# Splitting the SiLU of the last stage of a LayerNorm, convolution, attention and gate kernel into two activations

## The reference, cut to what matters

```
xn = layernorm(x)                                   # x: 2 x 4096 x 4096, f32
s  = attention(conv3(xn)) @ proj_w + proj_b         # conv 4096 -> 3*1024, 16 heads, blocks of 128 rows
g  = silu(xn * w_sum + w_dense @ expert_bias)       # top 8 of 64 router weights, w_sum their sum
x  = x + s * g
```

## Time and profile before

| what | value |
|---|---|
| median of 2 runs | 1908.17 us (1907.36 to 1908.99) |
| the profiled execution, its own time | 1908.72 us |
| span of its slowest core, core 1 | 1907.2 us |
| spans of the 8 cores | 1888.7 to 1907.2 us |
| PE busy | 1539.2 us, 81% of the span |
| DVE busy | 374.1 us, 20% |
| ACT busy | 381.8 us, 20% |
| POOL busy | 214.3 us, 11% |

### The profile page before, as it was taken

The page is one execution under the profiler, slowest core; times in us unless marked ns, Lnnn a source line. Parts: engine busy times, 40 slices in busy tenths (PEclk is TensorE's granted clock), DMA queues, the critical chain, the costliest instruction groups (busy, mean ns, idle before and its releaser), DMA issues.

```text
span 1907.2 us, 17823 instructions; the slowest of 8 cores (1888.7 to 1907.2 us)
## 1 busy us (share of the span) xinstructions
PE 1539.2 (81%) x7424; PEld 727.6 (38%) x7424; DVE 374.1 (20%) x644; ACT 381.8 (20%) x445; POOL 214.3 (11%) x180
## 2 busy tenths in 40 slices
PE   0345799999999999999999999886765773966780
PEld 0345344444444444444444444333443441311220
DVE  2776100000000000000000000003255231533543
ACT  1443000000000000000000000596345331423322
POOL 0000011111111111111111111000000000221133
PEclk9877799999999999999999999997555556876685
DMA  5997666666666666666666666441000048044224
GB/s 138 218 248 158 76 78 78 76 76 74 75 76 77 78 78 76 73 74 76 77 77 78 77 74 85 75 66 23 1 1 1 1 89 187 1 124 141 89 94 170
DMA packets 230821, 163.62 MB, mean 86 GB/s; under 512 B 74691, under 2 KB 222403, under 8 KB 226499
## 3 DMA queue, kind: packets, MB, share of 16 engines
q0 software_dynamic: 155472, 92.97, 38.4%
q1 hardware_dynamic: 75270, 69.50, 13.8%
HBM read 220.69 MB, written 16.78 MB: 125 GB/s over the span
## 4 chain that ended last, share of the span: by engine, by line
PE 61%; DMA 12%; DVE 10%; ACT 7%; POOL 3%; issue 3%; SPq 3%; POOLq 0%; DVEq 0%; ACTq 0%
PE pCv L632 53%; DMA AL<-x 7%; PE pWO L913 4%; DMA AL<-pw 4%; POOL AL L1047 2%; ACT AL L694 2%; DVE AL L787 1%; DVE AL L1030 1%; PE pQ L716 1%; DVE tStat L320 1%; SPq L416 1%; ACT AL L1042 1%; DVE tRs L779 1%; ACT L694 1%; POOL AL L1050 1%
## 5 line engine op out<-in xcount | busy, mean ns | idle before, releaser
L632 PE MATMUL pCv<-AL 128*128 128x512 bf16 x4608 | 1002.9, 380 | 1.0 <-DVE tWmT L550 1.0
L632 PEld LDWEIGHTS pCv<-AL 128*128 128x128 bf16 x4608 | 450.0, 98 | 553.8 <-issue 4.4
L765 DVE TENSOR_REDUCE tSc<-pS 128x1 f32<-128x512 f32 x32 | 21.8, 680 | 1189.9 <-PE pS L758 1189.9
L575 POOL DMA_DIRECT2D AL<-cw x144 | 125.9, 875 | 1053.4 <-PE pCv L632 863.0
L647 ACT ACTIVATE AL<-pCv,tCbT 128x512 bf16<-128x512 f32 x48 | 29.1, 688 | 889.2 <-PE pCv L632 889.2
L454 PE MATMUL pLgT<-AL 128*64 128x128 bf16 x768 | 62.0, 262 | 124.6 <-DMA AL<-AL 124.6
L982 PE MATMUL pPr<-AL 128*128 128x512 bf16 x448 | 120.8, 418 | 17.3 <-DVE AL L1030 17.3
L913 PE MATMUL pWO<-AL 64*128 64x256 bf16 x512 | 109.8, 414 | 5.7 <-DVE AL L839 5.7
L454 PEld LDWEIGHTS pLgT<-AL 128*64 128x64 bf16 x768 | 60.9, 141 | 125.5 <-issue 125.5
L913 PEld LDWEIGHTS pWO<-AL 64*128 64x128 bf16 x512 | 73.2, 144 | 41.4 <-issue 6.6
L799 PE MATMUL pPT<-tI,AL 128*128 128x128 bf16 x128 | 18.7, 301 | 73.1 <-DVE AL L787 73.1
(11 more groups left out here) (94 smaller groups left out, 843.4 us busy)
## 6 DMA issues: line engine op xcount, KB each, us to landing
AL<-cw POOLq DMA_DIRECT2D x144, 512.0 KB, 5.9
AL<-x SPq DMA_DIRECT2D x16, 2048.0 KB, 13.9
out<-AL SPq DMA_DIRECT2D x8, 2048.0 KB, 8.8
AL<-pw POOLq DMA_DIRECT2D x8, 1024.0 KB, 8.5
AL<-wq POOLq DMA_DIRECT2D x1, 2048.0 KB, 18.8
AL<-wk POOLq DMA_DIRECT2D x1, 2048.0 KB, 15.1
AL<-wv POOLq DMA_DIRECT2D x1, 2048.0 KB, 14.8
AL<-wo POOLq DMA_DIRECT2D x1, 2048.0 KB, 15.7
```

What stands on the lines that cost most here:

```text
L575: sCWs[gi % 4].add(e.dma_start(out=cwr[:, gi % 4, :].rearrange("p (g f) -> p g f", g=8), in_=d_cw[s, g].rearrange("g p f -> p g f")), 16)
L632: ins = e.matmul(p_cv[:, 512 * (bs + 2 * sub + hf): 512 * (bs + 2 * sub + hf) + 512], lhsT, xnTh[:, o:o + 512], start=(step == 0), stop=(s ...
```

## The change

SiLU of a tile is issued as two activations. The first covers columns 0 to 1535 and waits for the first three segments only (3 x 512 columns); the second covers columns 1536 to 4095 and waits for all eight. `cSIL` now goes up by two in a tile: POOL's product waits for the first activation, DVE's for the second.

```diff
                 @AC
                 def _(e, tt=tt):
+                    e.wait_ge(cGI.h, 8 * tt + 3)
+                    cSIL.add(e.activation(gw[:, 0:1536], gw[:, 0:1536], AF.Silu), 1)
                     e.wait_ge(cGI.h, 8 * (tt + 1))
-                    cSIL.add(e.activation(gw, gw, AF.Silu), 1)
+                    cSIL.add(e.activation(gw[:, 1536:4096], gw[:, 1536:4096],
+                                          AF.Silu), 1)
 
                 @GP
                 def _(e, tt=tt):
-                    e.wait_ge(cSIL.h, tt + 1)
+                    e.wait_ge(cSIL.h, 2 * tt + 1)
                     cPL.add(e.tensor_mul(s6[tt % 2][:, 0:1536], s6[tt % 2][:, 0:1536],
                                          gw[:, 0:1536]), 1)
...
                 @DV
                 def _(e, tt=tt):
-                    e.wait_ge(cSIL.h, tt + 1)
+                    e.wait_ge(cSIL.h, 2 * tt + 2)
                     dedge(e, e.tensor_mul(s6[tt % 2][:, 1536:4096],
```

## The result

The changed kernel is a little faster: its time against the kernel before has the ratio 0.9916, 95% interval 0.9891 to 0.994. That is 0.8%, or 16 us of 1908 (11 to 21 by the interval). The forecast was 18.2 us, a ratio of 0.9905. The median of all runs is 1898.1 us (1880.66 to 2097.79, 31 runs), beside 1912.8 for the kernel before, which was timed again with it; the three longest runs, above 2050 us, show a lower granted clock on the cores of one die and are left out of the ratio. The profiled execution took 1885.5 us, 23 less than the one of before. That is more than the ratio says; the excess is shorter loads, which other cores and other runs of the kernel before have as well.

What follows compares the result with a forecast made beforehand. Bound: a ring per tile of DVE's adds, SiLU, POOL's product and add, store and load of x, without PE. Saving 2.6 us in tiles 1 to 7, 18.2 off 1908.72, gave 1890.5, predicted as 1890; range 1874 to 1900.

Steps and rivals of the forecast that it cites:

- When POOL may start: After SiLU's first part: POOL's product starts 4.87 us behind the tile's first add (T) instead of 10.00.
- the straight line: SiLU time interpolated between 512 and 4096 columns, 0.834 ns a column: 1.48 us for 1536, 2.34 for 2560.
- What POOL meets there: DVE and POOL alternate: L1035, POOL's product, L1057, POOL's add end in turn; store and load start 2.6 us earlier.
- Behind it: After POOL's add: store and load move together, load time stays (median 14.5 us), PE's 4.3 of cover suffices.
- Sum: Whole kernel: 2.6 us saved in each of tiles 1 to 7, 18.2 in all, hence 1890 us.
- POOL wins the pair: Rival, chance 0.18: POOL's product runs before L1035, saving 5.1 us per turn, 32.6 in all, hence 1876.
- PE becomes the bound: Rival: PE at low clock needs a turn of at least 35.5 us, hence 1897; chance 0.12 together with somewhat slower loads.
- the 4.3 of cover: Time from PE's last matmul of tile 5 to ACT's table load at 1830.54; 2.6 us would eat only part.
- the 34.2 of that sum: PE's time in us for all eight segments at the low clock, part of the 35.5 us turn.
- The change doesn't do what it says: Rival, chance 0.02: something holds POOL until SiLU's second part is done; all stays within 2 us, 1907.
- The transfers take it back: Rival, chance 0.04: paired cores fall into step, loads of x take about 18.4 us, kernel 5 slower, 1913.

Runs made afterwards that it cites:

- the first experiment: The changed kernel with SiLU's first part also waiting for all eight adds; ratio to the kernel before 0.9959 (0.9918 to 1.00).

## Why the prediction was right

Step by step:

- *When POOL may start.* T+4.87 was forecast, T+4.88 measured. SiLU of 1536 and 2560 columns took 1.48 and 2.34, both as the straight line had it. There was no second table load.
- *What POOL meets there.* Four ends were forecast at T+7.61, 10.90, 13.58 and 16.85; they came at T+7.60, 10.89, 13.58 and 16.85. The half-length L1035 shows that the product waits for the rest of L1035, and the delayed L1035 shows that the earlier one runs whole.
- *Behind it.* SP's pair of transfers moved by the same 2.6, and ACT's copies still waited for the store, not for PE. The load itself, taken as it is with a median of 14.5, had one of 12.0 on the slowest core. The forecast has no term for that; by it the two profiled executions lie 23 us apart instead of 18.
- *Sum.* 18.2 forecast, 16 measured, with 11 to 21 by the interval. The saving is what was shown, seven times 2.6. The time of 1890 is less well founded: it starts from two runs with a median of 1908.2, and the median of 30 was 1912.8; and it falls between the two groups of the last section, with no run of the changed kernel within 4 us of it. The median of 1898.1 lies only 2 us inside the range of 1874 to 1900.

Of the rivals, "POOL wins the pair" was nearly as close as argued: the margin was 0.09 us in the changed kernel, and 0.18 more for DVE turned it. Its price was right per turn, 2.56 beyond the forecast where 2.5 was said; in sum it had 32.6 us off the kernel before, and by its ratio the run with the delayed L1035 has 26. "PE becomes the bound" did not happen, but it was nearer than the 4.3 of cover says, which is one tile of one core. The cover is the time from PE's last bias matmul (L990) to ACT's table load: before, it is 0.9 to 8.6 us, by core and tile; in the changed kernel 0.35 to 5.1. The 0.35 is on core 5, where PE ends at 1814.70 and the table load begins at 1815.05, behind 8.6 us at a granted clock of 0.50 to 0.52. (Eight segments at 4.3 us are 34.4, not the 34.2 of that sum; nothing hangs on it.) "The change doesn't do what it says" is out as well: POOL's product begins at 1795.73, before SiLU's second part at 1795.81. "The transfers take it back" was wrong in its price. I extrapolated 18.4 us for two cores in step; the nearest case seen, two cores that issue 0.2 to 0.4 us apart, has loads of 15.9 to 16.6. This is 4.6 more than a free load of 11.8, but only 2 more than the median of 14.5 on core 1 before. It stays below the 3.0 at which the gain would have been lost.

What the first experiment corrects is a reading that the forecast did not make but invites: that the early wait is where the gain comes from. The two parts alone, both started behind the last add, give most of it per turn: less the load, a turn takes 20.4 us there, against 20.0 with the early wait and 22.6 before.

## What to carry to other kernels

Where two engines exclude each other, count the time of their instructions in a row, as if they were one engine, and ask which of them must be finished for the next transfer to start; an earlier release is worth only what that row leaves free. Work that is not needed at that point (here the sum for the previous tile) belongs in the idle time ahead of it, and delaying it by 0.2 us was better than letting it win. Before shortening a ring that goes through a load, ask whether the load must be in it: taking the sums, the store and the load one tile earlier gave 3.6% without the split and 5.5% with it, against 0.8% for the split alone.

## What the runs showed of the hardware

**A waiting engine goes next.** In every turn looked at, DVE and POOL alternated: after POOL's product it was DVE's waiting instruction that ran, although POOL's add was ready, and the other way round. A margin of 0.04 to 0.09 us decided who came first. The Trainium skill, "SBUF — State Buffer", section "Who interferes with whom", says that issue order decides and that the second is blocked fully. These runs agree: the same L1035 takes 2.81 when it is issued 0.09 ahead of POOL's product, and 6.03 when issued 0.09 behind.

**Loads depend on the distance of two neighbouring cores.** Every load here is 2 MB behind a store of 2 MB. The execution with the delayed L1035 has both kinds. The line of the load, core 4, core 5, then core 0, us from issue to landing:

```profile
DMA to landing us min/median/max: 16.1/16.5/16.6
...
DMA to landing us min/median/max: 15.9/16.3/16.6
...
DMA to landing us min/median/max: 11.8/11.8/12.7
```

Cores 4 and 5 issue 0.2 to 0.4 us apart in all six tiles and both wait 15.9 us or more; cores 0 and 1 issue 11 us apart and wait 11.8 and 11.9 (medians). The distance is not all: the third load takes 12.7 and 13.1 on cores 0 and 1 too, and why is open. The spans are 1883 for cores 4 and 5 and 1855 to 1867 for the others. The two that are in step stay in step through the six tiles; both are slowed alike.

This also fits the spread of the whole times. Of the 28 runs of the changed kernel that the ratio uses, 11 lie from 1880.7 to 1885.5 us and 17 from 1895.6 to 1903.0; each of the 17 has a pair (0 and 1, 2 and 3, 4 and 5, or 6 and 7) whose spans differ by at most 4.3 us, with a mean of 1889 or more, and in the 11 no pair is closer than 4.9. The kernel before has the same two groups. Of its 23 runs that the ratios of the experiments use, 10 lie from 1900.0 to 1906.5 us, none with a pair closer than 4.9; of the 13 from 1907.3 to 1920.2, 12 have a pair at most 4.6 apart. So the groups are no effect of the change. The runs of the kernel before that the changed kernel's own ratio uses can be divided at 1907 us in the same way. Group beside group, the medians then differ by 16.9 us in the lower and by 15.5 in the upper; divided at their widest gap, 1909.0 to 1912.8, by 17.8 and 16.5. The forecast was 18.2. Both divisions were drawn afterwards.

That the pairs share a path to memory is an inference from this; no run here moved one core against its neighbour on purpose. Which group a run falls into is worth as much as the change. That fits a gain of 2.6 us per turn, seen without exception in the traces, which shows in the whole time only as 0.8% with an interval half a per cent wide.
